# Layer 1's experts: the order of three groups of loads on SyncE's queue, and half 1's norm behind five scatters instead of two

## The reference

```python
gate_logits = jnp.einsum('bsd,de->bse', x, Wg) + bg
gate_probs = jax.nn.softmax(gate_logits, axis=-1)
topk_probs, topk_idx = jax.lax.top_k(gate_probs, 2)
topk_probs = topk_probs / jnp.sum(topk_probs, axis=-1, keepdims=True)
weights = jnp.einsum('bske,bsk->bse', jax.nn.one_hot(topk_idx, 8), topk_probs)
h = jax.nn.gelu(jnp.einsum('bsd,edf->bsef', x, W1) + b1, approximate=False)   # f = 512
y = jnp.einsum('bsef,efd->bsed', h, W2) + b2
x = x + jnp.einsum('bsed,bse->bsd', y, weights)                               # x was normed on the way in
```

## Time and profile before

| what | us |
|---|---|
| median of 3 runs | 1211.0 (1207.81 to 1212.24) |
| the profiled execution, its own time | 1222.69 |
| its span, first to last instruction | 1221.0 |
| PE busy | 935.2, 77% of the span |
| DVE, ACT, POOL busy | 741.0, 604.0, 443.9 |
| mean granted clock of TensorE | 0.888 of full speed |
| layer 1's experts, the 30 tiles on PE | about 555 to 638 on the profile's axis |

### The profile page before, as it was taken

The page is one execution under the profiler, slowest core; times in us unless marked ns, Lnnn a source line. Parts: engine busy times, 40 slices in busy tenths (PEclk is TensorE's granted clock), DMA queues, the critical chain, the costliest instruction groups (busy, mean ns, idle before and its releaser), DMA issues. The chain is left out here.

```text
span 1221.0 us, 21718 instructions
## 1 busy us (share of the span) xinstructions
PE 935.2 (77%) x7744; PEld 689.3 (56%) x7744; DVE 741.0 (61%) x1800; ACT 604.0 (49%) x1671; POOL 443.9 (36%) x543
## 2 busy tenths in 40 slices
PE   6357877784879586856699998998878994387696
PEld 4324545343876245646695775676537883144496
DVE  4778886793414746752136864766677766685432
ACT  1148775572544555634356774777303223375143
POOL 3288773672223124534252331333420003111243
PEclk9779898996999798867799999999979998598588
DMA  8960000004355000034440000000203000000351
GB/s 254 187 70 1 1 1 19 1 2 136 117 178 216 33 1 2 19 89 127 129 147 19 1 2 1 1 2 2 117 1 138 1 1 18 0 1 1 101 166 46
DMA packets 73420, 71.73 MB, mean 59 GB/s; under 512 B 19752, under 2 KB 60321, under 8 KB 72001
## 3 DMA queue, kind: packets, MB, share of 16 engines
q1 hardware_dynamic: 69728, 62.70, 18.3%
q0 software_dynamic: 3584, 7.63, 1.8%
HBM read 54.90 MB, written 15.94 MB: 58 GB/s over the span
## 5 line engine op out<-in xcount | busy, mean ns | idle before, releaser
L2599 POOL TENSOR_TENSOR arena<-arena 128x512 f32<-128x512 f32 x64 | 66.7, 1042 | 151.5 <-DVE arena L2654 151.5
L2589 ACT ACTIVATE arena<-arena 128x128 f32<-128x128 f32 x256 | 99.2, 391 | 21.4 <-DVE arena L2617 21.1
L324 POOL TENSOR_TENSOR norm_rstd<-norm_std,minus_half 128x4 f32<-128x4 f32 x24 | 25.6, 1065 | 202.1 <-DVE norm_std L319 202.0
L1424 ACT ACTIVATE arena<-bank,w_L_ffn_b1T 128x128 f32<-128x128 f32 x192 | 54.7, 370 | 79.4 <-PE bank L1413 63.2
L1435 PE MATMUL bank<-bufB,arena 128*128 128x128 f32 x368 | 53.3, 292 | 14.9 <-ACT arena L1424 10.1
L2613 DVE SCALAR_TENSOR_TENSOR arena<-bank,bufA 128x512 f32<-128x512 f32 x64 | 43.8, 684 | 30.6 <-PE bank L2535 30.6
L1435 PEld LDWEIGHTS bank<-bufB,arena 128*128 128x128 f32 x368 | 49.0, 207 | 16.0 <-ACT arena L1424 10.8
L551 PE MATMUL bank<-arena 128*128 128x512 f32 x64 | 38.3, 690 | 20.7 <-DVE arena L511 18.8
L2918 ACT ACTIVATE arena<-bank 128x512 f32<-128x512 f32 x36 | 21.6, 599 | 61.3 <-PE bank L1193 61.3
L2454 PE MATMUL bank<-xnT,w_qkv 128*128 128x512 f32 x96 | 49.7, 617 | 1.6 <-ACT arena L378 1.6
L2506 PE MATMUL bank<-arena 128*64 128x128 f32 x512 | 42.1, 285 | 10.5 <-ACT arena L2580 10.3
(11 more groups left out here) (527 smaller groups left out, 2768.3 us busy)
## 6 DMA issues: line engine op xcount, KB each, us to landing
bufB<-in_L_ffn_w SPq DMA_DIRECT2D x28, 256.0 KB
bufA<-in_L_ffn_w SPq DMA_DIRECT2D x2, 2048.0 KB
bufB<-in_L_ffn_W SPq DMA_DIRECT2D x2, 2048.0 KB
arena<-in_L_ffn_W SPq DMA_DIRECT2D x16, 256.0 KB
bufB<-in_L_ffn_w SPq DMA_DIRECT2D x2, 2048.0 KB
bufA<-in_L_ffn_W SPq DMA_DIRECT2D x12, 256.0 KB
arena<-in_L_ffn_w SPq DMA_DIRECT2D x12, 256.0 KB
rows_one<-blank SPq DMA_DIRECT2D x4, 704.0 KB, 12.4
```

The source lines that it names most:

```text
L1424: o = act.activation(e["hidden"][n % 3][:, f, :], banks[2 + n % 3][:, f * P:(f + 1) * P], ACT.Gelu, bias=b1[:, f:f + 1])
L2589: o = act.activation(tile, tile, ACT.Exp, bias=b2["mn"][n % 8][:, j:j + 1], scale=-1.0, accum_out=b2["sm"][n % 8][:, j:j + 1])
L2599: pool.tensor_tensor(tile, tile, bc(b2["rs"][n % 4], 2, P), ALU.mult).then_inc(g["over_sum"].sem, 1)
```

## The change

On SP all seven shared tiles' weights of half 0 come ahead of half 0's rows, and half 1's rows come right behind half 0's rows, ahead of half 1's shared weights. On POOL half 1's norm step comes behind scatter 4 (five scatters) instead of behind scatter 1 (two). No instruction is added or removed.

```diff
@@ layer1_experts_loads
             sync.dma_start(e1_b2, d["L1_ffn_b2"]...)
-            sparse_extra(sync, e1, 0, range(4), range(4))
+            sparse_extra(sync, e1, 0, range(EXTRA), range(4))
             rows_load(0)
-            sparse_extra(sync, e1, 0, range(4, EXTRA), range(4))
+            rows_load(1)
             sparse_extra(sync, e1, 1, range(4), range(4))
-            rows_load(1)
             back_load(0)
             sparse_extra(sync, e1, 1, range(4, EXTRA), range(4))
@@ layer1_experts_pool
             for j in range(8):
                 scatter_two_pool(pool, 0, j)
-                if j == 1:
+                if j == 4:
                     rstd_pool(pool, "L1_ffn", 1)
             second_rows_pool(pool, 1)
```

## The result

| | median us | runs |
|---|---|---|
| before | 1210.77 (1203.09 to 1216.08) | 19 |
| changed | 1202.99 (1195.96 to 1209.96) | 19 |

Ratio 0.9935, 95% interval 0.9913 to 0.9957: 7.8 us faster. The forecast was 1205.3, 5.7 us faster. The profiled execution of the changed kernel took 1196.31 us, 26.4 us less than that of before. That is far more than the medians differ, so most of it is not the change. To compare stages I count from POOL's first scatter of half 0, at 535.39 before and 532.53 after, the last thing ahead of the change.

What follows compares the result with a forecast made beforehand. PE was taken to be bound by two waits for rows loaded from HBM, 12.6 us together, the longer on the path. Terms -12.2 + 6.5 + 0 = -5.7 us gave 1205.3 us from the median 1211.0, range 1197.5 to 1211.5.

Steps and rivals of the forecast that it cites:

- Part 1: Half 1's rows ahead of its shared weights on SP: PE's 10.21 us wait and slow restart go, gain 12.2 us.
- The room: At half 1's first turn: rows arrive by 580.7, PE wants them at 591.95, so 11 us to spare.
- Rival D: Half 1's rows stay late behind POOL's scatters and SP's queue; only the loss remains: 1217.5 us, chance 0.07.
- Part 2: All seven shared tiles' weights ahead of half 0's rows on SP: rows arrive later, loss 6.5 us, bounds 4.0 and 8.0.
- the 1.39 at 545.73: SP's hold-up in before's profile: 1.39 us for a DMA that else takes 0.33.
- the way from ask to turn: Half 0's rows: asked for at 556.15, taken to arrive at 561.8; before, 3.15 us on an idle queue.
- The clock that rises later: At half 0's later start, the clock's rise may move by a few us at half speed: 0 to 1.5 us.
- My working by bytes: 4.58 MB of weights and scatters at 205 to 221 GB/s end at 557.7 to 559.3; half 0's rows 3.3 us later.
- Part 3: Half 1's norm step behind five scatters on POOL: not delayed, scatters end 3.8 us earlier, worth nothing; up to 2.4 otherwise.
- A: Half 0's rows come quicker, the weights ahead being nearly through: loss 4.0 instead of 6.5 us, 1202.8 us, chance 0.15.
- C: SP held up by its own queue, 1.1 us in each of five shared tiles: 5.3 us more, 1210.6 us, chance 0.13.
- B: ACT's stops before tiles 4 and 5 go with overlapping weight transfers: up to 9.2 us more back, 1196.1 us, chance 0.12.

Runs made afterwards that it cites:

- The two repeats on one chip: Before and the changed kernel, both unaltered, each profiled again on the second chip: 1202.67 us (one run) and 1202.58 us (ratio 0.9944).
- changed kernel's repeat: The changed kernel once more, unaltered, on the second chip: 1202.58 us, ratio 0.9944 against before.
- the first pair: The original profiled executions of before and of the changed kernel: 1222.69 and 1196.31 us.
- the lighter weights: Changed kernel with W1 and W2 of half 0's shared tiles 4 to 6 loaded on 16 of 128 partitions only: 1205.33 us, one run.
- before's repeat: The kernel before, unaltered, profiled once more on the second chip: 1202.67 us, one run.
- rows early: Against before, half 1's rows asked for ahead of its shared weights, half 0's shared tiles still split: 1213.33 us, ratio 0.9873; with norm step behind five scatters 1211.65 us, 0.9853.
- the first set: Follow-up runs on the chip where before took 1228.11 us: rows of half 1 early with and without the norm step's move, seven shared tiles first, norm step alone.
- the run with the loss alone: Against before, only all seven shared tiles of half 0 ahead of its rows: 1235.75 us, ratio 1.0068.
- the norm step alone: Against before, only half 1's norm step moved behind five scatters: 1227.66 us, ratio 0.9986.
- Part 1 and part 3 without part 2: Against before, half 1's rows early and norm step behind five scatters, half 0's shared tiles still split: 1211.65 us, ratio 0.9853; repeated on the second chip 1192.78 us, 0.989.
- the scatters ahead of result 0 besides: Against before, half 1's rows early, norm step behind five scatters, all eight half 1 scatters ahead of result 0: 1192.25 us, ratio 0.986; repeated 1191.55 us, 0.9877.

## Why the prediction was right

The two repeats on one chip give the terms without ACT's stops: a gain of 12.9 us and a loss of 6.3, together 6.5, where 12.2, 6.5 and 5.7 were forecast. The medians' 7.8 us have an interval of 5.2 to 10.5, which holds the stage's 6.5; the 1.3 between them are not explained and need not be more than noise.

**Part 1, the gain: right.** The wait was on the path and went whole, and nothing took its place: half 1's rows were asked for when its scatters had landed, and PE met no new wait for weights or results behind them. On the stop-free pair, from half 0's last turn to half 1's first is 590.69 - 574.49 = 16.20 us before and 589.59 - 583.90 = 5.69 after, 10.5 less; the next turn follows after 9.94 instead of 7.58 us, 2.4 more of slow restart (granted clock 0.50 from 589 to 595, 1.00 in the changed kernel's repeat). That is 12.9 us against 12.2 forecast; the first pair gives 12.2 the same way.

The room was far smaller than I had it, 11 us. The changed kernel asked for half 1's rows at 577.14 and turned them at 584.65, 7.51 us later (582.01 and 589.59, 7.58 us, in its repeat), and with the 5.27 us that I allowed for the load 2.2 us of room are left. The 11 us counted the time of ACT's stops, which only some profiles have. In the run with one scatter ahead of each result the room was used up, and 1.58 us of wait came back. Rival D was nearer than the prediction thought.

**Part 2, the loss: right in its mechanism, 0.4 to 1.3 us too large.** Forecast were rows asked for 4.03 us later, their arrival 5.65 us after that, and 6.5 us in all. The start moved from 19.88 to 25.05 in the first pair, 5.2 us, and in the stop-free pair from 19.53 to 25.64, 6.1 us. Up to half 0's last turn this loss was 583.90 - 536.66 - (574.49 - 533.59) = 6.3 us; with the gain of 12.9 that gives the stage's 6.5. Two terms were a little too large. One is SP's: I placed the rows' load 20.76 us after the first scatter (556.15), and it was at 20.04 and 20.43. In the first pair that is because the three added tiles took 7.2 us, not 7.65, and because the one hold-up was 1.14 us, not the 1.39 at 545.73. The other is the way from ask to turn: 5.01 and 5.21 us where I had 5.65. The clock that rises later cost 0.2 us (first to second turn 6.44 us against 6.20), within the 0 to 1.5 that I had put into the range.

The Trainium skill ("DMA: Bandwidth & Descriptors", section "Queues, rings and completion order") states that each DMA engine takes a queue's descriptors in ring order. What the runs show agrees, but its price is small: fewer bytes ahead of the rows gave 0.7 to 0.9 us, while the greater part of the loss is SP's issuing. My working by bytes fits the changed kernel: 234 GB/s from 534.1 to 554.0 are 4.66 MB, near the 4.58 MB of weights and scatters, and the turn came 3.58 us after 554.0, where I had 3.3. But by the same working the lighter weights should have let the rows come in about 3.2 us, and they took 4.36. So bytes do not explain the whole way from ask to turn, and that its forecast came so near is in part luck.

**Part 3, worth nothing: right here, but my bound was too wide.** The norm step was not delayed. But if the load could follow the scatters, I had let the start go forward by 2.4 us, until PE's counts end. DVE's slots and owners end later than that and hold the first copy: the first up product came only 0.5 us (21.43 in before's repeat to 20.96 with rows early, on one chip) to 1.1 us (22.10 to 20.96 on the other) earlier.

**The rivals.** A (quicker rows) did not come: 5.0 to 5.2 us from ask to turn, and a loss of 5.2 to 6.1. C (SP held up) was seen on the first set's chip in the run with the loss alone, 2.1 us more than the changed kernel's ask. D did not come, but the room that kept it off was the small one above. B is the one that a reader of one pair of profiles would have believed: the stops were there before and gone after. Before's own repeat has none, so it takes no change to lose them; and the run with the loss alone has them with the weights landed. So the first pair is no evidence that the change removes them. The changed kernel itself has no profile on the first set's chip, so that it would keep them there is likely (each of its parts does) and not shown. The stops are why the profiled pair differs by 16.6 us in this stage, where the medians differ by 7.8 in all.

**What stays open.** The stops themselves: all four profiles of the first set have them and none of the eight on the second chip. Whether they belong to the chip or to an execution, and why ACT stands still with PE's product made, was not tried further. Open too are the 1.2 to 1.5 us that lighter weights do not take off the rows' way. The first set's parts are also larger than on the second chip: -15.6 us for the rows where the stage gives 12.9, +8.4 for the weights where the start moved by 7.65; the intervals (about 3.5 us each side) allow it. One pair of profiles on the first chip tells a little more: the norm step alone took 100.45 us for the stage and the same with rows early 88.59, so rows early are worth 11.9 us in the stage there, near the forecast, though the ratios of these two differ by 16 us. In these two profiles the rest of the difference lies outside the stage, where the kernels are the same.

**A better version.** Part 1 and part 3 without part 2 were 0.9853 and 0.989, with the scatters ahead of result 0 besides 0.986 and 0.9877, where the changed kernel had 0.9935 and 0.9944. These beat both kernels; between the two of them, 1.3 us apart on one chip, nothing can be told.

## What to carry to other kernels

When a load that is ready stands behind one that waits on a queue, moving it forward gains the whole wait and the slow restart behind it, 12.9 us here. But price what goes ahead of the other load in the same edit, in issue time of the queue first: 7.2 us of DMAs ahead of half 0's rows, 3.3 to 3.7 of them beyond what SP had stood idle, gave back 5 to 6 us. And before a stop that is in one profile and not in the other is put down to a change, the unchanged kernel is profiled a second time.

## What was not expected of the hardware

- ACT stood idle 3 to 6 us with PE's product made, twice within 11 us, in some profiles (the first at tile 4, 15 to 18 us after half 0's first turn), and DVE with it, the weights having landed in the run with the loss alone. In others the same kernel had none, even where POOL issued 19 indirect DMAs without a pause of over 0.5 us (564.56 to 587.64 in the changed kernel).
- The same kernel took 1228.11 us on one chip and 1208.63 on another, 1.6% apart, more than twice the change.
